# Inverse and scaled keys come back from DRAM in one 64 KB load, with padded scratch and a refitted engine order

## What is computed

```python
x_act = jnp.tanh(x)
static_out = jnp.einsum('bld,ed->ble', x_act, W)
q = k = to_heads(x_act); v = to_heads(static_out)     # 8*16 heads, 2048 steps, 16 wide
def step(S, inp):
    k_t, v_t, q_t = inp
    S = lam * S
    u = beta * (v_t - jnp.einsum('kv,k->v', S, k_t))
    S = S + k_t[:, None] * u[None, :]
    return S, jnp.einsum('kv,k->v', S, q_t)
y = static_out + o_dyn                                 # then a layer norm with gamma and beta
x = _layernorm(x + attn(x))
x = _layernorm(x + down(silu(x @ Wg.T) * (x @ Wu.T)))
```

## Time and profile before

| | |
|---|---|
| median of 3 runs | 1834.14 us (1823.91 to 1838.68) |
| profiled execution | 1828.82 us, its span 1827.0 us |
| TensorE busy | 1387.4 us (76%) |
| VectorE busy | 1423.6 us (78%) |
| ScalarE, GpSimd busy | 1099.6 us (60%), 784.0 us (43%) |
| DMA packets, SP's queue | 700288, 187.55 MB, 49.7% of 16 engines |
| granted TensorE clock, mean | 0.848 |

### The profile page before, as it was taken

One profiled execution on the slowest core, in us unless ns is written; L12 is line 12 of the kernel. 1 busy time (PEld: TensorE's weight loads), 2 busy tenths in 40 slices (PEclk: granted clock), 3 DMA queues, 4 the chain that ended last, 5 costly groups with the idle time before them and its releaser, 6 DMA issues.

```text
span 1827.0 us, 53670 instructions
## 1 busy us (share of the span) xinstructions
PE 1387.4 (76%) x21032; PEld 1075.2 (59%) x21032; DVE 1423.6 (78%) x3479; ACT 1099.6 (60%) x2339; POOL 784.0 (43%) x1106
## 2 busy tenths in 40 slices
PE   1254888788888878887888788788888878888764
PEld 0244666666666656666666566666666666666542
DVE  8267888888888888887888888787888887878741
ACT  0233666666756666666666666676666666766544
POOL 6012444445444444454444444444434435444442
PEclk9855888888998888889898888898988888988877
DMA  2455555555555455555655565455445665454200
GB/s 69 82 105 112 98 110 121 116 109 116 114 117 108 105 119 121 107 117 114 114 110 106 113 122 109 110 116 113 104 107 118 124 106 116 113 112 97 67 24 24
DMA packets 700541, 190.98 MB, mean 105 GB/s; under 512 B 620160, under 2 KB 687744, under 8 KB 700288
## 3 DMA queue, kind: packets, MB, share of 16 engines
q1 hardware_dynamic: 700288, 187.55, 49.7%
HBM read 103.55 MB, written 67.11 MB: 93 GB/s over the span
## 4 chain that ended last, share of the span: by engine, by line
SPq 30%; PE 22%; DMA 19%; DVE 13%; issue 8%; ACT 7%; POOL 1%; ACTq 0%; POOLq 0%; DVEq 0%
PE pc L175 9%; SPq L977 8%; DMA scr_t<-t 6%; SPq L938 6%; SPq L947 6%; SPq L986 5%; DMA scr_x<-xt 3%; PE pd L272 3%; SPq L992 3%; DMA scr_g<-gs 2%; PE pf L220 2%; PE pu L246 2%; DMA y_out<-v 2%; PE pf L209 2%; DMA xa<-L_attn_x 2%
## 5 line engine op out<-in xcount | busy, mean ns | idle before, releaser
L879 POOL TENSOR_TENSOR hlo<-gate,hhi 128x512 f16<-128x512 f32 x192 | 228.7, 1193 | 327.9 <-ACT hhi L710 327.5
L175 PE MATMUL pc<-R,tb 128*128 128x32 f16 x4096 | 158.1, 189 | 158.9 <-DVE R L362 139.3
L175 PEld LDWEIGHTS pc<-R,tb 128*128 128x128 f16 x4096 | 147.2, 118 | 178.3 <-DVE R L362 154.0
L175 PE MATMUL pc<-S,e 128*128 128x32 f16 x4096 | 157.1, 186 | 66.9 <-DVE S L383 66.8
L175 PEld LDWEIGHTS pc<-S,e 128*128 128x128 f16 x4096 | 151.6, 118 | 84.2 <-DVE S L383 77.0
L209 PEld LDWEIGHTS pf<-xb,e 128*128 128x128 f16 x4096 | 152.4, 118 | 64.7 <-DMA e<-scr_x 47.6
L209 PE MATMUL pf<-xb,e 128*128 128x32 f16 x4096 | 156.2, 191 | 41.3 <-DMA e<-scr_x 39.9
L272 PE MATMUL pd<-wd_t,hhi 128*128 128x256 f16 x768 | 175.4, 275 | 13.9 <-DVE xr L481 8.5
L175 PEld LDWEIGHTS pc<-U,kb 128*128 128x128 f16 x4096 | 154.0, 118 | 52.8 <-DVE U L370 50.6
L175 PE MATMUL pc<-U,kb 128*128 128x32 f16 x4096 | 159.8, 190 | 26.4 <-DVE U L370 26.4
L272 PE MATMUL pd<-wd_t,hlo 128*128 128x256 f16 x768 | 175.1, 275 | 0.0
(11 more groups left out here) (118 smaller groups left out, 3280.1 us busy)
## 6 DMA issues: line engine op xcount, KB each, us to landing
xa<-L_attn_x SPq DMA_DIRECT2D x128, 128.0 KB
scr_x<-xt SPq DMA_DIRECT2D x64, 256.0 KB, 2.1
xb<-scr_x SPq DMA_DIRECT2D x256, 64.0 KB, 2.9
e<-scr_x SPq DMA_DIRECT2D x256, 64.0 KB, 3.7
scr_g<-gs SPq DMA_DIRECT2D x32, 512.0 KB
gh<-scr_g SPq DMA_DIRECT2D x32, 512.0 KB, 4.0
kb<-k SPq DMA_DIRECT2D x512, 32.0 KB, 2.3
scr_t<-t SPq DMA_DIRECT2D x64, 256.0 KB
```

The costliest lines, as they stand in the source:

```text
L175: last = pe.matmul(pc2[:, :, cols], stationary(h, a), moving[:, :, cols], start=a == 0, stop=a == 1)
L879: pool.tensor_tensor(hlo[:, t, :], gate[:, t % 2, :], hhi[:, t, :], ALU.subtract).then_inc(SEM["hl"], 1)
```

## The change

`tb` and `kb` become two halves of one buffer `tk`. The scaled keys no longer go from SBUF to SBUF: `sp_store_scaled` stores `k16` to a DRAM scratch `scr_tk` beside the inverse (one transfer of 256 KB for each g, in pieces of 128 bytes, semaphore kd0 or kd1), and `sp_load_blocks` brings inverse and scaled keys back together, by 8 transfers of 64 KB (semaphore tk0 or tk1) in place of 16 of 32 KB. `pe_keys_by_update` has no wait of its own for its operand any more. `k16` is now free when the store has landed. `scr_tk` is single: both stores of a half wait until the last load of that half has landed. The rows of `scr_g` and the heads of `scr_tk` get one sequence of padding, 9 in place of 8, so `scr_g`'s rows are 36 KB apart (32 KB before) and heads in `scr_tk` 18 KB. All five engine orders are written anew.

```diff
-        tb = sb("tb", [P, 2, H, B, C, 2, 2], F16)
-        kb = sb("kb", [P, 2, H, B, DH, 2, 2], F16)
+        tk = sb("tk", [P, 2, 2, H, B, C, 2, 2], F16)
+        tb, kb = tk[:, :, 0], tk[:, :, 1]
...
-        scr_g = nc.dram_tensor("scr_g", [C, B, H, T], F32).ap()
-        scr_t = nc.dram_tensor("scr_t", [B, 2, H, C, T], F16).ap()
+        scr_g = nc.dram_tensor("scr_g", [C, B + 1, H, T], F32).ap()[:, 0:B]
+        scr_tk = nc.dram_tensor("scr_tk", [2, 2, H, B + 1, C, T], F16).ap()[:, :, :, 0:B]
...
         def pe_keys_by_update(pe, q, p, w):
             pe.wait_ge(SEM["u"], n_of("u", q, w + 1))
-            if w % 2 == 0:
-                pe.wait_ge(SEM[f"kb{w // 2}"], n_of(f"kb{w // 2}", q))
...
-            act.wait_ge(SEM[f"kb{g}"], n_of(f"kb{g}", q - 1))
+            act.wait_ge(SEM[f"kd{g}"], n_of(f"kd{g}", q - 1))
...
+        def sp_store_scaled(sp, q, p, g):
             sp.wait_ge(SEM["k16"], n_of("k16", q, g + 1))
             sp.sem_inc(s_hop, 1)
+            sp.wait_ge(SEM[f"tk{g}"], n_of(f"tk{g}", q - 1))
+            sp.dma_start(scr_tk[g, 1].rearrange("h b i t -> (b i) h t"),
+                         k16[:, g].rearrange("p h k z m -> p h (k z m)")).then_inc(SEM[f"kd{g}"], 16)
+
+        def sp_load_blocks(sp, q, p, g):
+            sp.wait_ge(SEM[f"kd{g}"], n_of(f"kd{g}", q))
+            sp.sem_inc(s_hop, 1)
             sp.wait_ge(SEM["sp"], n_of("sp", q - 1, 2 * g + 2))
+            sp.sem_inc(s_hop, 1)
+            sp.wait_ge(SEM[f"td{g}"], n_of(f"td{g}", q))
             for b in range(B):
+                sp.dma_start(tk[C * b:C * (b + 1), g, :, :, b].rearrange("j a h i z m -> j (a h) (i z m)"),
+                             scr_tk[g, :, :, b].rearrange("a h j t -> j (a h) t")).then_inc(SEM[f"tk{g}"], 16)
...
             if live(s - 2):
-                pe_up(pe, s - 2, p, 2)
-                pe_gate(pe, s - 2, p, 3)
-            if live(s + 1):
-                pe_gram(pe, s + 1, 1 - p, 0, range(0, 8))
+                pe_gate(pe, s - 2, p, 4)
+            if live(s):
+                pe_keys_by_state(pe, s, p, 0)
```

More of the change, by code:

```diff
@@ L310, in pe_step @@
             if live(s + 1):
+                pe_gram(pe, s + 1, 1 - p, 3, range(0, 8))
                 pe_gram(pe, s + 1, 1 - p, 3, range(8, 16))
@@ L345, in pe_step @@
                 pe_transpose_x1(pe, s - 1, 1 - p, 1)
+            if live(s):
+                pe_keys_by_state(pe, s, p, 3)
+            if live(s - 1):
+                pe_up(pe, s - 1, 1 - p, 0)
+                pe_gate(pe, s - 1, 1 - p, 0)
+            if live(s):
+                pe_inverse_by_rest(pe, s, p, 3)
+            if live(s - 1):
+                pe_gate(pe, s - 1, 1 - p, 1)
+                pe_gate(pe, s - 1, 1 - p, 2)
+                pe_up(pe, s - 1, 1 - p, 1)
             if live(s):
@@ L579, in dve_step @@
             if live(s):
-                dve_state(dve, s, p, 3)
+                dve_rest(dve, s, p, 3)
             if live(s + 1):
                 dve_invert(dve, s + 1, 1 - p, range(11, 13))
+            if live(s + 2):
+                dve_scale_keys(dve, s + 2, p, 0)
+            if live(s + 1):
+                dve_invert(dve, s + 1, 1 - p, range(13, 15))
+            if live(s - 1):
+                dve_multiply(dve, s - 1, 1 - p, 0)
+            if live(s):
+                dve_update(dve, s, p, 3)
+            if live(s + 1):
+                dve_store_inverse(dve, s + 1, 1 - p, 0)
+            if live(s - 1):
+                dve_multiply(dve, s - 1, 1 - p, 1)
+            if live(s):
+                dve_state(dve, s, p, 3)
+                dve_statistics(dve, s, p, 2)
+            if live(s + 2):
+                dve_scale_keys(dve, s + 2, p, 1)
+            if live(s - 1):
+                dve_multiply(dve, s - 1, 1 - p, 2)
         def act_rest(act, q, p, w):
@@ L773, in act_step @@
                 act_update(act, s, p, 1)
+            if live(s + 2):
+                act_activate(act, s + 2, p)
             if live(s - 2):
@@ L786, in act_step @@
                 act_variance(act, s - 1, 1 - p, 2, 0)
+                act_variance(act, s - 1, 1 - p, 2, 1)
+            if live(s):
+                act_decay(act, s, p, 2)
+            if live(s - 1):
+                act_variance(act, s - 1, 1 - p, 2, 2)
+                act_variance(act, s - 1, 1 - p, 2, 3)
+            if live(s + 1):
+                act_static_out(act, s + 1, 1 - p, 0)
             if live(s):
@@ L1005, in sp_step @@
                 sp_store_keys(sp, s + 1, 1 - p, 1)
+            if live(s):
+                sp_store_scaled(sp, s, p, 1)
+            if live(s + 1):
                 sp_spread_packed_keys(sp, s + 1, 1 - p)
                 sp_spread_keys(sp, s + 1, 1 - p)
+            if live(s):
+                sp_store_inverse(sp, s, p, 0)
             if live(s - 1):
@@ L1098, in _ @@
             eng.memset(as_u32(E[1][:, :].rearrange("p z h b i n -> p (z h b i n)")), 0).then_inc(s_pool0, 1)
-            eng.memset(as_u32(tb[:, :].rearrange("p g h b i z m -> p (g h b i z m)")), 0).then_inc(s_pool0, 1)
-            eng.wait_ge(s_pool0, 14)
+            for g in range(2):
+                eng.memset(as_u32(tb[:, g].rearrange("p h b i z m -> p (h b i z m)")), 0).then_inc(s_pool0, 1)
+            eng.wait_ge(s_pool0, 15)
             eng.wait_ge(s_c, N_SETUP)
```

237 lines of the change are left out of this document (92 added, 145 removed).

## The result

The changed kernel takes 1980.45 us, the median of 4 runs (1977.79 to 1982.95), where the kernel before, run beside it, takes 1833.64. The ratio is 1.081, with a 95% interval of 1.076 to 1.086: 147 us slower, 4.6 us for each of the 32 steps. The forecast was 93 us faster. The profiled execution took 1982.15 us, its span 1980.3.

What follows compares the result with a forecast made beforehand. The loop from xt by `e` to the gram was to bound: 48.4 plus 0.2 us for extra traffic, 48.6 against 51.5; 2.9 us over 32 steps takes 93 off 1828.8, so 1736 us, range 1700 to 1790.

Steps and rivals of the forecast that it cites:

- SP is the fullest engine: SP's queue before the change: 43.6 us of each 51.5 us step is issuing; the change leaves about 31.5.
- three loops: Loops from xt to xt: by SP to the inverse 47.4 us, by `e` to the gram 48.4, VectorE alone 46.3.
- Rival 2: No change: single-buffer waits replace SP; gram's way 10.0 us, 2.4 more gives pitch 51.0 and 1813 us; chance 0.12.
- The common end: Stretch from wave 0's update to the next xt, shared by the loops: 24.4 us before, 22.3 after the change.
- Loop A's front: From xt ready through SP's queue to the landing of the inverse's loads: 23.4 us.
- Loop B: From xt by `e` to the gram and on to the next xt: 48.4 us, 48.6 with extra traffic.
- Extra traffic: Scaled store's 2048 pieces of 128 bytes ahead of `xb`: `e` later by 0.1 to 1.7 us, taken as 0.2.
- the waits of SP for xt: SP's queue after the change: it should wait for xt some 5 us or more in each step.
- the wait behind the second scaled store: SP's wait after that store: about 3 us, at no cost on the path because the gram isn't ready that early.
- Rival 3: Slower: DRAM writes in 128-byte pieces at twice 25 ns delay `e` by 4.9 us; pitch 53.3, 1887 us; chance 0.10.
- idle time before L369 in wave 1: VectorE's wait between rest and update of wave 1, no longer covered by key norms: near 1.6 us.
- L: Theory in the experiments' expectations, not the prediction: latencies through DRAM close the loop.

Runs made afterwards that it cites:

- e1: d1 with SP's four loads of x moved ahead of the gram's store; 1857.38 us, ratio 1.020 to the kernel before.
- d1: Changed kernel with a buffer of its own for the output (gamma added in place of beta); 1932.48 us, ratio 1.058.
- e2: b4 with the half-1 scaled store moved behind the next step's `e` loads; 1922.90 us, ratio 1.055.
- b4: Kernel before with the scaled keys alone sent through DRAM, 32 KB loads at their old places; 1882.58 us, ratio 1.029.
- d2: Kernel before with a buffer of its own for the output (gamma added in place of beta); 1822.29 us, ratio 0.996.
- b1: Kernel before with the last gram product ahead of the first inverse product, and the gram stored ahead of the scaled keys' half 1; 1962.05 us, ratio 1.071.
- b5: b4 with b1's move of the last gram product and the gram's store; 1946.72 us, ratio 1.064.
- b3: a4 with inverse and keys loaded apart, half 0's keys ahead of the gram's store and half 1's behind its load; 1962.03 us, ratio 1.071.
- c1: Changed kernel with x loaded ahead of the gram's store, the gram's load directly behind it, then the second inverse store; 1973.36 us, ratio 1.079.
- a1: Changed kernel without padding of the gram's rows; 1976.15 us, ratio 1.084.
- c3: Changed kernel with half 0 loaded in two groups of 32 KB loads, inverse first, then scaled keys; 1975.69 us, ratio 1.080.
- a3: Changed kernel with `gh` loaded directly behind the gram's store, and x last, behind the second inverse's store; 2040.5 us, ratio 1.119.
- c2: c1 with a buffer of its own for the output (gamma added in place of beta); 1867.54 us, ratio 1.022.
- d3: c2 with the last gram product first and the gram's store ahead of x; 1938.28 us, ratio 1.061.
- a4: Kernel before's order with the new path: common buffer, scaled keys through DRAM, 64 KB loads, padding; 1895.69 us, ratio 1.039.
- d4: b4 with a buffer of its own for the output (gamma added in place of beta); 1881.80 us, ratio 1.030.

## Why the prediction was wrong

**The step that failed is the list of loops.** "SP is the fullest engine" was true, and its chain through SP's queue was read rightly; but what would bound once SP was relieved was taken from three loops that all close at xt. The gram's way back, from its store over its landing and its load to the mask and the next inverse, was in none. In the kernel before, SP's issuing hid two of its joints, and at the mask it was waited for in 7 of 23 steps, 5.9 us in all, so it looked harmless. In the changed kernel SP waits for the gram 3.4 us a step, for its landing 2.0, and VectorE for `gh` 5.2, in every step, and this loop is 56.3 us long in place of the forecast 48.6. e1 shows that these legs carry time: one move that shortens them by 2.5 us a step wins 75 us.

**The round trip was mis-sized where it was counted.** Rival 2 gave it 10.0 us from wave 0's update to landing: 1.4, seven issues at up to 0.66 (4.6), and 4.0. It took 16.5 (913.53 to 930.00): 2.1 to the store's issue, 8.6 until SP may issue the load, and 5.8 to the mask. The middle leg isn't set by the issues in it, which end 2.2 us sooner, but by the store's own landing, which SP waits out, and it had been left out. Rival 2 then added 2.4 us where 6.5 were missing; even so it named the right place.

**The common end** was put at 22.3 us plus 1.65. In the changed kernel it runs from the product with the inverse at 911.87 to xt ready at 943.0, 31.1 us, since the mask stands in it and waits 5 us for `gh`, and ScalarE then waits for the output. The prediction had the mask cover a wait of 1.00; in fact the mask was moved ahead of its own data.

**The output's landing** was in no step. d1 puts its worth at 48 us.

**Loop A's front** was nearly right: 23.4 us forecast, 25.3 measured (xt ready at 886.55, first product at 911.87). Of the missing 1.9 us, 0.7 is the issuing of `xb` and `e` (9.0), 0.85 a wait until the inverse is ready, and 0.9 a longer landing of the inverse; the rest is small or goes the other way. From the inverse's store to its product it takes 13.1 us (898.81 to 911.87), before 11.0 (879.68 to 890.64), and this part stands in the gram's loop as well.

**Loop B** was named as the bound, and its sign failed: TensorE's gram was to wait for `e` in most steps, and from 400 to 1600 us it did so for 5.0 us in all, in at most 7 of 21 steps.

**Extra traffic** was costed at 0.2 us on `e`. For `e`'s landing that holds (3.7 before and after). What struck was a transfer's place among the others: `gh` close behind the second inverse's store, and in e2 the residual and the inverse behind the scaled keys.

**Right were** the waits of SP for xt (over 5 us a step: 7.6), the wait behind the second scaled store (53.6 / 22 = 2.4, forecast about 3, and free), the scaled store's landing of 3.4 us (2 to 4), and the padding at zero. Also right were 52 transfers a step and an idle time before L369 in wave 1 near 1.6 us (1.75 at 924.10). Rival 3, small writes dear enough to make `e` late, is refuted for the changed kernel by the 3.4 and by `e`'s 3.7; the change is slower by another way than the one it named. A milder price of the detour remains, in b4's 5.6 and 52 us.

**The balance**, by the kernels on record: of the 147 us, 48 vanish with the output's own buffer (d1), 75 more with x ahead of the gram's store (e1), and e1 is still 2.0% over the kernel before (by the ratios 41, 70 and 37 us). Its column in the table is 0.9 us longer: 2.3 more in the first leg, where inverse and keys are stored, loaded in 64 KB and waited for together, 1.2 less from mask to inverse, the rest small. What of this costs the 2.0% was not tested. None of the runs is faster than the kernel before by over 0.4% (d2), and d2 leaves beta out.

Three things stay open. L expected a gain in the old order from an earlier gram (b1, b5) or an earlier inverse (b3), and each time another wait grew instead: ScalarE's for `kb` in b1, TensorE's for `tk` in b3 (63.2 us, 30 times), ScalarE's for x in b5 (63.7 us in 22 steps). How much each of these costs was only read, not tested. The detour's 52 us in b4 are shown as a sum, not by place. And x ahead of the gram's store was not tried without the output's own buffer, so how much that one move would give the changed kernel is not known; c1, which moves the gram's load too, won 7 us.

## What to carry to other kernels

Follow one chain from an instruction to the same instruction a step later, and list every such loop that passes through a store, its landing and a load back; how full a queue is doesn't tell which part of it bounds, and taking work from one place of it, which is one run, tells of that place. A round trip that is waited for in few steps isn't harmless: it may end just before it is needed (0.3 us in the median for `gh` in the kernel before), and any new order can bring it onto the path. With nearly equal bounds side by side, test fixes in pairs, since each alone shows a fraction (7 and 48 us here, against 113 together). And try loads that can be issued early ahead of a large store in the same queue: here that one move was worth 75 us.

## What the runs showed of the hardware

- Issuing stretches behind a large store: four loads of x took 2.67 us to issue ahead of the gram's 512 KB store (e1) and 4.9 behind it (changed, d1).
- `gh`'s 512 KB landed in 5.8 to 6.0 us (medians) where a 256 KB store had been issued 2.8 us before it (changed, d1, a1, c3), and in 3.9 to 4.4 where that store was some 5.9 us ahead (e1) or behind it (a3, c1, c2, d3). That the one causes the other is read from these runs. x's loads moved in some of them too, but they seem the smaller part: with x behind the gram's store and the inverse's store behind the load (d3), it was 4.4, and 3.9 with x ahead (c2).
- Rows 36 KB apart in place of 32 made no difference, 6.0 against 5.8 us and 4.0 against 4.0.
- A 256 KB store to DRAM in 128-byte pieces landed in 3.3 to 3.5 us in the new orders and in 4.8 to 5.6 in the old one (a4, b3, b4, b5, d4, e2); the keys' 256 KB store `scr_x`, in longer pieces, in 2.2 (changed).
